# Moving decay factors, skips, norms and value copies to ScalarE and the decayed state to VectorE in an mLSTM mixer with a mixture of experts

## The reference

```python
x_mlstm, z = split(x @ W_up)
x_act = swish(causal_conv(x_mlstm, 4 taps) + conv_b)
q, k, v = headwise(x_act, Wq), headwise(x_act, Wk), headwise(x_mlstm, Wv)
ig, fg = gates(q, k, v)
logD = (cumsum(log_sigmoid(fg)) differences, lower triangle) + ig
mD = max(logD, axis=-1)
Dmat = exp(logD - mD)
C = q @ k.T * DH ** -0.5 * Dmat
h = (C / (max(abs(C.sum(-1)), exp(-mD)) + 1e-6)) @ v
hn = per-head layernorm(h) * norm_w
out = ((hn + skip * x_act) * swish(z)) @ W_down
```

## Time and profile before

| | |
|---|---|
| median of 3 runs | 886.41 us (883.32 to 891.37) |
| profiled execution | 881.61 us, of it the span 879.9 us |
| mean granted TensorE clock | 0.963 of full speed |
| busy: TensorE, weight loads | 789.5 us (90%), 665.3 us (76%) |
| busy: VectorE | 658.6 us (75%) |
| busy: GpSimd | 372.1 us (42%) |
| busy: ScalarE | 363.2 us (41%) |
| transfers | 81.01 MB, mean 92 GB/s |

### The profile page before, as it was taken

How to read it: one execution, slowest core, us unless ns; L and a number is a source line. 1 busy time by engine, 2 the same in 40 slices (tenths; PEclk the granted TensorE clock), 3 DMA queues, 4 the chain that set the end, 5 groups by cost and what they waited for, 6 DMA issues and landing times.

```text
span 879.9 us, 17647 instructions
## 1 busy us (share of the span) xinstructions
PE 789.5 (90%) x5783; PEld 665.3 (76%) x5783; DVE 658.6 (75%) x1711; ACT 363.2 (41%) x621; POOL 372.1 (42%) x370
## 2 busy tenths in 40 slices
PE   6879967599999999999999999999999999999966
PEld 5656656488887888887878787878787878787855
DVE  5799953577777787777777777777777777778754
ACT  4757732234344344343343434343434343433231
POOL 5050018542635363636353545463535454544200
PEclk8999977689999999999999999999999999999979
DMA  4878744210404040404040404040403040400000
GB/s 119 242 244 278 272 164 129 95 49 25 131 24 131 24 131 24 131 24 131 24 131 24 132 24 131 24 131 24 131 24 131 24 131 24 131 24 25 1 12 13
DMA packets 53104, 81.01 MB, mean 92 GB/s; under 512 B 10176, under 2 KB 36952, under 8 KB 49112
## 3 DMA queue, kind: packets, MB, share of 16 engines
q1 hardware_dynamic: 53080, 80.68, 29.8%
HBM read 55.24 MB, written 25.43 MB: 92 GB/s over the span
## 4 chain that ended last, share of the span: by engine, by line
PE 38%; DVE 20%; issue 17%; DMA 11%; POOL 7%; SPq 2%; ACT 2%; POOLq 1%; DVEq 1%; ACTq 0%
DMA max_b<-max_scratch 11%; PE bank L1395 10%; PE bank L1366 5%; DVE acc L838 5%; PE bank L1370 4%; PE bank L1367 4%; PE bank L1339 3%; DVE st L990 3%; PE bank L1385 3%; DVE out_sb L1002 2%; POOL D L548 2%; POOL D L538 2%; DVE Y L1002 2%; POOL kept L567 2%; PE bank L1315 2%
## 5 line engine op out<-in xcount | busy, mean ns | idle before, releaser
L754 ACT ACTIVATE s_in<-bank 128x512 f32<-128x512 f32 x144 | 86.1, 598 | 178.5 <-PE bank L1370 177.6
L1395 PEld LDWEIGHTS bank<-ewout,h 128*128 128x128 f32 x1024 | 132.8, 191 | 8.6
L1366 PE MATMUL bank<-yT_hi,in_hi 128*128 128x512 f32 x288 | 128.8, 447 | 11.2 <-DVE h L1097 11.2
L552 POOL TENSOR_TENSOR rs<-ve,half 128x4 f32<-128x4 f32 x32 | 32.7, 1020 | 241.9 <-DVE ve L998 241.9
L1395 PE MATMUL bank<-ewout,h 128*128 128x128 f32 x1024 | 134.8, 275 | 0.0
L1097 DVE TENSOR_TENSOR h<-s_in,bank 128x512 f32<-128x512 f32 x144 | 98.1, 681 | 48.0 <-PE bank L1370 44.3
L538 POOL TENSOR_TENSOR D<-a_tok,max_b 128x512 f32<-128x512 f32 x64 | 65.5, 1044 | 120.4 <-DVE max_b L910 67.8
L1370 PE MATMUL bank<-yT_lo,in_hi 128*128 128x512 f32 x288 | 114.8, 398 | 0.0
L1367 PE MATMUL bank<-yT_hi,in_lo 128*128 128x512 f32 x288 | 114.4, 397 | 0.0
L1101 DVE TENSOR_TENSOR h<-h,bank 128x512 f32<-128x512 f32 x128 | 87.2, 681 | 14.4 <-PE bank L1385 14.4
L951 DVE TENSOR_TENSOR state<-kept,bank 64x130 f32<-64x130 f32 x128 | 36.6, 286 | 62.6 <-POOL kept L567 41.5
(11 more groups left out here) (193 smaller groups left out, 1643.7 us busy)
## 6 DMA issues: line engine op xcount, KB each, us to landing
xact_scratch<-xact SPq DMA_DIRECT2D x16, 1024.0 KB, 5.0
max_b<-max_scratch SPq DMA_DIRECT2D x15, 1024.0 KB, 7.6
xa<-xact_scratch SPq DMA_DIRECT2D x16, 512.0 KB, 6.4
silu_z<-xact_scratch SPq DMA_DIRECT2D x16, 512.0 KB, 3.7
inter_w<-inter_scratch SPq DMA_DIRECT2D x30, 256.0 KB, 7.5
x_in<-in_L_attn_x_dram SPq DMA_DIRECT2D x16, 256.0 KB, 4.8
xt_scratch<-x_t SPq DMA_DIRECT2D x16, 256.0 KB, 5.0
xT<-xt_scratch SPq DMA_DIRECT2D x16, 256.0 KB, 8.1
```

The source lines that it names most:

```text
L754: act.activation(s_in[:, j % 2], bank[4][:], ACT.Silu).then_inc(silu_done, 1)
L1366: pe.matmul(o, in_hi[:, m, j], yT_hi[:], start=True, stop=False)
L1395: i = pe.matmul(bank[7][:, k * P:(k + 1) * P], h2[:, j % 2, k * P:(k + 1) * P], w, start=(j == k == 0), stop=(j == NJ), skip_group_check=True)
```

## The change

- ScalarE computes the decay factors straight from `max_b`: 16 Exp of 128x128, each with a column of `a_tok` as its bias and the scale -1, in place of 4 of 128x512. GpSimd then fills the upper triangle with 0 instead of -1e30. `args` is gone.
- `kept` is gone. VectorE updates the state with four scalar_tensor_tensor of 64x65 (state times decay plus update) in place of two additions of 64x130.
- The skips are made by ScalarE, in slot 1.
- Both norms are made by ScalarE as `Identity(scale * x + bias)`, four instructions each. VectorE makes the bias, `nb = -mean * rs` (`shift`), where it made the norm. `Y` is normalised at the end of ScalarE's turn, `out_sb` in the next turn's `ffn_head`, between `yT_hi` and `ge`.
- The second half of the values is copied by ScalarE too.
- Turn 1 is taken out of the loop, since it has no earlier `out_sb` to normalise in its head.

```diff
             mix(0, None)
-            with eng.Fori(1, NG - 1) as g:
+            mix(1, 0)
+            with eng.Fori(2, NG - 1) as g:
                 mix(g, g - 1)
...
             def mix(g, f):
-                sp.wait_ge(arg_sub, nth(g, 4, 3))
+                sp.wait_ge(D_exp, nth(g, 4, 3))
...
-            def args(g, kp):
...
+            def masks(g):
+                for q in range(4):
+                    pool.wait_ge(D_exp, nth(g, 4, q))
                     alone(pool)
-                    d = D[:, kp, par].rearrange("p k s t -> p (k s) t")
-                    pool.affine_select(out=d, in_=d, compare_op=ALU.is_ge, fill=masked, base=0,
-                                       pattern=[[0, 2 * NP], [1, P]], channel_multiplier=-1).then_inc(arg_masked, 1)
+                    d = D[:, q // 2, q % 2].rearrange("p k s t -> p (k s) t")
+                    pool.affine_select(out=d, in_=d, compare_op=ALU.is_ge, fill=zero, base=0,
+                                       pattern=[[0, 2 * NP], [1, P]], channel_multiplier=-1).then_inc(D_done, 1)
...
-                    pool.tensor_tensor(kept[:], state[:], dec[:, k, :].unsqueeze(2).to_broadcast([P, NP, 2 * DV]),
-                                       ALU.mult).then_inc(kept_done[k], 1)
...
-                    if k < NP:
-                        pool.tensor_scalar(mixed[:, k], xa[:, k], vecs[:, k, VS:VS + 1], None, ALU.mult
-                                           ).then_inc(skip_done, 1)
-                    if k in (1, 2) and not (isinstance(g, int) and g == NG - 1):
-                        args(g + 1, k - 1)
...
+                if not (isinstance(g, int) and g == NG - 1):
+                    masks(g + 1)
                 pool.wait_ge(ve1_done, g + 1)
                 power(rs1[:], ve1[:], rs1_done)
...
+                act.wait_ge(val_mm[1], g + 1)
+                copy(vals[:, 2:4, :, 0:DH].rearrange("p k h d -> p (k h) d"),
+                     bank[0][:].rearrange("p (q d) -> p q d", d=DH)).then_inc(val_out[1], 1)
 
             def decays(g):
...
                 for q in range(4):
-                    act.wait_ge(arg_masked, nth(g, 4, q))
-                    d = D[:, q // 2, q % 2].rearrange("p k s t -> p (k s t)")
-                    act.activation(d, d, ACT.Exp).then_inc(D_done, 1)
+                    kp, par = q // 2, q % 2
+                    if q == 0:
+                        act.wait_ge(max_in, 16 * (g + 1))
+                    prev(act, C_done[kp][par], g)
+                    for k in range(2 * kp, 2 * kp + 2):
+                        for h in range(par, NH, 2):
+                            i = act.activation(D[:, kp, par, k % 2, h // 2], max_b[:, h, k * P:(k + 1) * P], ACT.Exp,
+                                               scale=-1.0, bias=a_g[:, k, h:h + 1])
+                    i.then_inc(D_exp, 1)
...
+                    if j == SKIP_SLOT:
+                        act.wait_ge(xa_in, 16 * (g + 1))
+                        prev(act, down_mm, g)
+                        for p in range(NP):
+                            act.activation(mixed[:, p], xa[:, p], ACT.Copy, scale=vecs[:, p, VS:VS + 1]
+                                           ).then_inc(skip_done, 1)
...
                 if not last:
                     mix_front(g + 1)
+                mixer_norm(g)
+
+            def normalise(dst, src, rs, nb, s):
+                for k in range(NC):
+                    i = act.activation(dst[:, k], src[:, k], ACT.Identity, bias=nb[:, k:k + 1], scale=rs[:, k:k + 1])
+                i.then_inc(s, 1)
...
                 copy(yT_hi[:], bank[7][:]).then_inc(yT_hi_done, 1)
+                if before(f) is not None:
+                    ffn_norm(before(f))
                 act.wait_ge(logit_mm, f + 1)
...
             def update_state(g, k):
                 dve.wait_ge(upd_mm[k], g + 1)
-                dve.wait_ge(kept_done[k], g + 1)
+                if k:
+                    dve.wait_ge(state_done[k - 1], g + 1)
+                else:
+                    prev(dve, state_done[NC - 1], g)
...
-                    i = dve.tensor_tensor(state[r, :, c], kept[r, :, c], new[r, :, c], ALU.add)
+                    for s in range(NP):
+                        i = dve.scalar_tensor_tensor(state[r, s, c], state[r, s, c], now[r, s:s + 1], new[r, s, c],
+                                                     ALU.mult, ALU.add)
...
-            def normalise(dst, src, mv, rs, s):
-                for k in range(NC):
-                    i = dve.tensor_scalar(dst[:, k], src[:, k], mv[:, k, 0:1], rs[:, k:k + 1], ALU.subtract, ALU.mult)
-                i.then_inc(s, 1)
+            def shift(nb, mv, rs, s):
+                dve.scalar_tensor_tensor(nb[:], mv[:, :, 0], -1.0, rs[:], ALU.mult, ALU.mult).then_inc(s, 1)
...
+SKIP_SLOT = 1
```

More of the change, by code:

```diff
@@ L153, in mixer_moe_block @@
         state = sb("state", [P, NP, 2 * DV])
-        kept = sb("kept", [P, NP, 2 * DV])
         p1 = ExitStack()
@@ L267, in mixer_moe_block @@
         rs2 = sb("rs2", [P, NC])
+        nb1 = sb("nb1", [P, NC])
+        nb2 = sb("nb2", [P, NC])
         out_sb = sb("out_sb", [P, NC, E])
@@ L326, in groups, with before @@
             ffn(NG - 1)
+        def before(f):
+            return None if isinstance(f, int) and f == 0 else f - 1
         def prev(eng, s, g, per=1):
@@ L599, in _ @@
             pool.wait_ge(back_out, 1)
-            args(0, 0)
             weigh_queries(0)
-            args(0, 1)
+            masks(0)
             pool.wait_ge(back_out, BACK)
@@ L735, in mix, with mixer_norm, ffn_norm @@
                     mix_front(g + 1)
+                mixer_norm(g)
[3 more added lines that the diff above has]
+                i.then_inc(s, 1)
+            def mixer_norm(g):
+                act.wait_ge(nb1_done, g + 1)
+                act.wait_ge(z2_done, g + 1)
+                normalise(Y, y1, rs1, nb1, Y_done)
+            def ffn_norm(f):
+                act.wait_ge(nb2_done, f + 1)
+                prev(act, out_stored, f, 16)
+                normalise(out_sb, z2, rs2, nb2, out_done)
             def ffn_head(f):
@@ L946, in update_state @@
                 dve.wait_ge(upd_mm[k], g + 1)
[L947 removed]
+                if k:
+                    dve.wait_ge(state_done[k - 1], g + 1)
+                else:
+                    prev(dve, state_done[NC - 1], g)
+                now = decay[:].rearrange("p s (g k) -> p g k s", k=NC)[:, bass.ds(g, 1), k].rearrange("p g s -> p (g s)")
                 new = bank[0][:, 0:NP * 2 * DV].rearrange("p (s d) -> p s d", s=NP)
@@ L1110, in ffn_norm @@
                 dve.wait_ge(rs2_done, f + 1)
-                prev(dve, out_stored, f, 16)
-                normalise(out_sb, z2, mv2, rs2, out_done)
+                shift(nb2, mv2, rs2, nb2_done)
             def ffn(f):
```

43 lines of the change are left out of this document (11 added, 32 removed).

## The result

| | before | after |
|---|---|---|
| median | 888.4 us (4 runs, 883.3 to 891.4) | 912.1 us (4 runs, 911.1 to 916.9) |
| ratio after to before | | 1.028, 95% interval 1.022 to 1.035 |
| profiled execution, its span | 881.6, 879.9 us | 911.1, 909.4 us |
| mean granted TensorE clock | 0.963 | 0.944 |
| busy: TensorE, VectorE, ScalarE, GpSimd | 789.5, 658.6, 363.2, 372.1 us | 800.6, 622.3, 465.0, 219.0 us |

The changed kernel is 2.8% slower. The forecast was 897 us with a range of 883 to 912: the direction was right, the growth was more than twice the one forecast (23.7 us between the medians for 10.6).

A forecast was written before the change was run, and what follows sets the result against it. Bound by a chain of other engines in each period's head, plus the max_b wait: 10.5 us for 14 periods, 0 start, 3 tail, 13.5 on 881.6 gives 895; a third of 4.8 more makes 897 us, range 883 to 912.

The forecast's parts named there:

- the start: First group: ScalarE's faster Y repays about 2 us lost to 16 exponentials; zero, give or take 1.5 us.
- the masks: GpSimd's masks follow each quarter of the exponentials and cost nothing; VectorE needs the first only behind Y, 3 us later.
- the state update: VectorE's four instructions take 0.93 us, 0.35 more; on the chain once, before the second chunk, the three others in gaps.
- the values: Second half's copy moves from VectorE to ScalarE, starting at 441.03 and ending at 441.63, as TensorE delivers.
- The tail: Last feed-forward, nothing covers the chain: 2.5 us for late s_in and 0.5 for the last norm, 3 us.
- The term of the head: From y to TensorE's second chunk: 1.74 us from late s_in plus 0.35 for the state, 2.1 us later.
- The shortest period, 42.82: Taken as the period with the max_b wait at nothing; removing the wait wins 1.34 us a period, 18.8 in all.
- GpSimd relieved: VectorE's small operations ran slower beside GpSimd's; beyond out_sb leaving VectorE, already in the sum, nothing more is counted.
- rival 4: Dearer: no overlap between ScalarE's short operations, state update at 1.2 us; head grows 3 us, 905 to 915 us; chance 0.14.
- The last step of the forecast: Chances against a 1% band, 877.5 to 895.3 us: faster 0.08, within 0.34, slower 0.58.
- rival 2: Head grows only about 1.4 us, second pointer free and state update overlapping; 882 to 891 us; chance 0.26.
- the first: Rival that the head grows by about 2.1 us and more than eats the wait; 892 to 904 us; chance 0.52.

The follow-up runs named there:

- x4: Changed kernel without the four masks on GpSimd, only the semaphore passed on: 906.9 us, 1.022 of the kernel before.
- x10: Changed kernel with the last of the four masks behind GpSimd's first power instead of ahead of it: 902.4 us, 1.019 of the kernel before.
- x5: Changed kernel with the decayed state made by GpSimd again and two additions of 64x130 on VectorE: 901.8 us, 1.021 of the kernel before.
- x7: Kernel before with only the decay factors changed, made by ScalarE from the loaded maxima, masks of zero behind: 872.8 us, 0.985 of the kernel before.
- x3: Kernel before with only the load of max_b issued earlier, within the turn before: 879.3 us, 0.992 of the kernel before.
- x9: Kernel before with only the two norms moved to ScalarE: 905.9 us, 1.025 of the kernel before.
- x6: Changed kernel with the first group's masks of quarters 2 and 3 behind GpSimd's memsets: 910.1 us, 1.026 of the kernel before.
- x11: Changed kernel with norms on VectorE, kept and skips on GpSimd, last mask later, first group's masks 2 and 3 behind memsets: 868.5 us, 0.981 of before.
- x1: Changed kernel with the norm of out_sb back on VectorE, behind yT_lo: 893.1 us, 1.009 of the kernel before.
- x12: Changed kernel, norms and second values on VectorE, kept on GpSimd, last mask later, first masks 2 and 3 behind memsets: 853.8 us, 0.964 of before.

## Why the prediction was wrong in size

Three steps failed: the start, put at zero, cost 5.8 us; the masks, said to "cost nothing", cost 4 us; and the state update, counted once, cost another 2 us a second time; together 12 of the 16.0 us missed.

**Right.** The direction; that the head grows and more than eats the wait; that `Y` and `out_sb` on ScalarE are its main terms. The four ACTIVATEs with two pointers took 1.65 us (forecast 1.60), the 16 Exp 4.79 (4.7), with `keyT` right behind them; `s_in` came 12.58 us behind `y` (12.2 to 12.5, and 0.3 of it is the mask); the values cost nothing in the periods. The state update in the head is 0.38 us longer (0.35). The tail was 3.7 us (3.0): 2.98 up to the last `z`, 0.74 for the last norm.

**The term of the head** was 2.1 us and measured 2.50. Without state and mask it grew by 1.82 (forecast 1.74). The rest is the step "the masks on GpSimd ... cost nothing": it asked only when VectorE needs the masks, not what runs beside them. The last mask slowed `ve`: 0.30 us a period, 4 us in all (x4, x10). The prediction had the earlier trace rows for this, small operations slow beside GpSimd's, and used them for the relief alone.

**The state update** stood in the sum once, "on the chain once", with the three others in gaps. The second is not in a gap: 0.16 us in the rest (x5), 2 us in all.

**The shortest period, 42.82.** With the two points above, 42.82 + 2.71 = 45.53 is what ran, for 44.9 forecast, so the sum holds by its own terms (0.40 in the head, 0.21 in the rest, 0.05 more in the mean for one fall of the clock; 14 times 0.66 is 9.3 us, with the rounding of the forecast 9.5, of the 16 us missed). But its frame, "that is the whole prize of taking it away", does not say what a part is worth: 1.34 would be 0.92 with the decay factors alone (x7), 0.46 in the mean by the early load (x3), 0.40 with the norms already moved (x9).

**The start**, "zero, give or take 1.5", was 5.8 us. The step looked at `Y` and at the 16 exponentials, and not at GpSimd's queue: its memsets stand behind four masks that now wait for those exponentials, and a copy of values came ahead of them. The first chunk is 2.2 us late by it; masks 2 and 3 behind the memsets give 2.1 of that back (x6). Another 1.4 us stand already at the copy of the maxima, within its spread. The remaining 2.2 us are a balance: 4.0 more from the first chunk to the first `y`, which go with TensorE at 1.2 GHz through the whole first group, where before came back to 2.4, and 1.8 less from there to the second `y`. No row of before announced the lower level, and its cause stays open. With 0.7 us of the tail these terms make up the 16.0 us between 13.5 and 29.5.

**GpSimd relieved, "nothing more".** No run tests this in the changed kernel. Where `out_sb` stays on VectorE, the skips alone are worth 0.40 us a period (x11): on GpSimd they slow that norm (2.16 us for 1.39).

**The rivals.** The time fell into the range of rival 4, but not by its mechanism: the ACTIVATEs do overlap and the update takes 0.97 us, not 1.2. That the time is only 0.1 us above the range says little: the range had no term for the start. The last step of the forecast also has its chances wrong: rival 2 and a quarter of the first are 0.26 + 0.13 = 0.39, not 0.34, which leaves 0.53 and not 0.58 for slower.

## What to carry to other kernels

A row in which a wait happens to be zero is not the kernel without that wait: ask what else was elsewhere in that period, and test by removing the wait alone (x3) and by the rest of the change alone (x9). Price what is moved on GpSimd by what runs beside it on VectorE, and walk each queue's first turn as well as its steady one. Of this change, the part that shortens GpSimd's work is worth having, and the norms are better left on VectorE: 853.8 us, 3.6% under the kernel before.

## What was not expected of the hardware

- A VectorE addition of 128x4 took 0.63 us beside one GpSimd mask of 0.64, and 0.17 when that mask stood 1.2 us later (changed kernel, x10).
- One idle time of 1.4 us in front of four transposes is followed, in some periods and not in others of equal shape, by TensorE at half its clock for some 7 us (x1: 2.44 us lost); that the idle time brings it is not shown. The same matmuls of the first group kept TensorE busy for 18.3 us in the changed kernel and 10.2 in x12.
- ScalarE's ACTIVATE of 128x128 with pointers for scale and bias: four in 1.65 us. The page "ScalarE: Activation LUTs" of the Trainium skill, section "What ACT_TABLE_LOAD costs", gives times by width and by pointer from which 1.64 was estimated; the rows agree.
- A switch of ScalarE's tables cost 1.28 us and nothing around it: `ge` ends at 460.51, the load starts at 460.53 and `s_in` at 461.82.
